# Layer norm of every stage: normalised rows made by ScalarE with a scale and a shift instead of by VectorE

## What is computed

```python
def _layernorm(x, axis=-1, eps=1e-05):
    m = jnp.mean(x, axis=axis, keepdims=True)
    v = jnp.var(x, axis=axis, keepdims=True)
    return (x - m) / jnp.sqrt(v + eps)

x = x + masked_attention(_layernorm(x))     # 16 heads of 16, T = 1024
x = x + ffn(_layernorm(x))                  # shared part of width 1024, 8 routed experts, top 2
x = x + gated_convolution(_layernorm(x))    # inner width 512, 4 taps
x = x + ffn(_layernorm(x))                  # the same weights again
x = x + selective_scan(_layernorm(x))       # 256 channels, 16 states
x = x + moe(_layernorm(x))                  # 16 routed experts, top 2
x = x + grouped_query_attention(_layernorm(x))  # 32 query heads, 4 key heads of 128
x = x + moe(_layernorm(x))
```

## Time and profile before

| | |
|---|---|
| median of 3 runs | 1946.65 us (1946.47 to 1948.49) |
| time of the profiled execution | 1946.17 us |
| its span, first to last instruction | 1944.3 us |
| PE busy | 1562.1 us (80%) |
| DVE busy | 1295.5 us (67%) |
| ACT busy | 932.3 us (48%) |
| POOL busy | 715.9 us (37%) |
| mean granted TensorE clock | 0.894 of 2.4 GHz |
| ACT's table loads (ACT_TABLE_LOAD) | 10, of 1.283 us each; none within a norm |

### The profile page before, as it was taken

How to read it: one execution, slowest core, us unless ns; L and a number is a source line. 1 busy time by engine, 2 the same in 40 slices (tenths; PEclk the granted TensorE clock), 3 DMA queues, 4 the chain that set the end, 5 groups by cost and what they waited for, 6 DMA issues and landing times. The chain is left out here.

```text
span 1944.3 us, 28391 instructions
## 1 busy us (share of the span) xinstructions
PE 1562.1 (80%) x9276; PEld 1214.6 (62%) x9286; DVE 1295.5 (67%) x2160; ACT 932.3 (48%) x2281; POOL 715.9 (37%) x735
## 2 busy tenths in 40 slices
PE   6899789878974655292769999999999999997372
PEld 4444568666851223281758888888888888885372
DVE  3665364766467998644647777777777778775743
ACT  2365335233524331251546666666666666663341
POOL 3011243324367764644832222222222222220743
PEclk9899799889987887595889999999999999999586
DMA  3320323222310001364000000000000000000443
GB/s 75 53 50 2 96 84 109 66 87 87 106 48 0 0 0 56 117 128 141 11 1 12 12 12 2 22 1 23 1 23 1 22 1 12 1 1 19 152 108 107
DMA packets 62059, 90.04 MB, mean 46 GB/s; under 512 B 10192, under 2 KB 44240, under 8 KB 61920
## 3 DMA queue, kind: packets, MB, share of 16 engines
q1 hardware_dynamic: 53664, 65.68, 11.4%
q0 software_dynamic: 8256, 22.56, 5.1%
HBM read 62.38 MB, written 19.40 MB: 42 GB/s over the span
## 5 line engine op out<-in xcount | busy, mean ns | idle before, releaser
L1294 DVE TENSOR_REDUCE gqa_neg_max<-acc 128x1 f32<-128x1024 f32 (+7 forms) x256 | 193.1, 754 | 173.2 <-PE acc L1403 172.1
L1180 ACT ACTIVATE gqa_probsT_high<-aux 128x512 fp32r<-128x512 f32 x288 | 172.0, 597 | 249.5 <-PE aux L1411 248.6
L1299 DVE TENSOR_TENSOR gqa_probsT_low<-aux,gqa_probsT_high 128x512 fp32r<-128x512 f32 x288 | 197.8, 687 | 29.8 <-ACT gqa_probsT_high L1180 25.6
L1189 ACT ACTIVATE gqa_probs<-acc,gqa_neg_max 128x1024 f32<-128x1024 f32 (+7 forms) x256 | 189.3, 739 | 29.6 <-DVE gqa_neg_max L1294 24.6
L1411 PE MATMUL aux<-ident,gqa_probs 128*128 128x128 f32 x1152 | 174.4, 274 | 0.0
L1087 POOL TENSOR_SCALAR gqa_q_scale<-gqa_q_scale 128x4 f32<-128x4 f32 x64 | 16.3, 255 | 381.0 <-ACT gqa_square L1124 380.7
L1422 PE MATMUL aux<-gqa_probsT_high,gqa_v_high 128*128 128x512 f32 x288 | 146.7, 509 | 1.0 <-DVE gqa_probsT_low L1299 1.0
L472 POOL DMA_INDIRECT f_xs<-tokens,f_slot_token x108 | 104.4, 967 | 108.4 <-PE aux L752 44.3
L1091 POOL TENSOR_TENSOR gqa_ln_xn<-gqa_ln_xn 128x512 f32<-128x512 f32 x64 | 82.2, 1285 | 147.0 <-DVE gqa_ln_xn L1219 146.9
L1434 PE MATMUL aux<-gqa_wo,gqa_oT 128*128 128x256 f32 x512 | 132.4, 381 | 4.4 <-DVE stream L1287 3.5
L1401 PE MATMUL acc<-gqa_k_low,gqa_q_high 128*128 128x512 f32 (+5 forms) x384 | 132.1, 344 | 0.0
(11 more groups left out here) (411 smaller groups left out, 4444.9 us busy)
## 6 DMA issues: line engine op xcount, KB each, us to landing
f_w<-in_f_up SPq DMA_DIRECT2D x64, 256.0 KB, 3.2
outputs_by_slot<-f_y_tile SPq DMA_DIRECT2D x108, 128.0 KB, 2.5
f_w<-in_f_down SPq DMA_DIRECT2D x64, 128.0 KB, 3.6
mat_qk<-mat_high SPq DMA_DIRECT2D x64, 64.0 KB, 2.3
tokens<-f_ln_xn SPq DMA_DIRECT2D x4, 1024.0 KB, 4.6
gqa_w_q<-in_g_wq SPq DMA_DIRECT2D x8, 512.0 KB, 3.6
gqa_wo<-in_g_wo SPq DMA_DIRECT2D x8, 512.0 KB, 3.8
mat_qk<-mat_low SPq DMA_DIRECT2D x32, 64.0 KB, 2.3
```

The lines of the kernel that those rows point to most:

```text
L1180: act.activation(probsT_high[:, u % RING, :], aux[:, u % 2, :], ACT.Copy).then_inc(cell_high_ready, 1)
L1189: act.activation(out, scores(n), ACT.Exp, bias=neg_max[:, j % (2 * JOBS):j % (2 * JOBS) + 1], accum_out=row_sum[:, n // 2 % 4, m, n % 2:n ...
L1294: dve.tensor_reduce(neg_max[:, j % (2 * JOBS):j % (2 * JOBS) + 1], scores(n), AXY, ALU.max, negate=True).then_inc(max_ready, 1)
L1299: dve.tensor_tensor(probsT_low[:, u % RING, :], aux[:, u % 2, :], probsT_high[:, u % RING, :].bitcast(F32), ALU.subtract).then_inc(cell_lo ...
```

## The change

The normalised tile is written by ACT, as `Identity(scale * x + bias)` with scale `rstd` and bias `shift` = -mean * rstd, both one value in each partition. POOL makes the shift: it negates the mean and multiplies it by `rstd`, two more small instructions for each pair (eight more for each layer). DVE's list becomes all statistics and then all low parts. ACT's list of the norm becomes, for each pair, the two `xn` tiles and then the `xnT_high` copy of the pair before. In the feed-forward layers ACT's `split(0)` moves from ahead of the norm to behind it. In masked attention ACT's norm moves ahead of the wait for the weights and their upper parts.

```diff
+        self.shift = sb("ln_shift", [P, NT])
+        self.mean_negated = sem("mean_negated")
+        self.shift_ready = sem("shift_ready")
...
-        def scale(q):
-            dve.wait_ge(self.rstd_ready, q + 1)
-            for t in (2 * q, 2 * q + 1):
-                dve.tensor_scalar(self.xn[:, t, :], c.x[:, t, :], self.mv[:, t, 0:1], self.rstd[:, t:t + 1],
-                                  ALU.subtract, ALU.mult).then_inc(self.xn_ready, 1)
...
-        for q in range(NT // 2 + 3):
-            if q < NT // 2:
-                statistics(q)
-            if 1 <= q < NT // 2 + 1:
-                scale(q - 1)
-            if q >= 3:
-                low(q - 3)
+        for q in range(NT // 2):
+            statistics(q)
+        for q in range(NT // 2):
+            low(q)
...
             pool.tensor_scalar(self.rstd[:, two], self.mv[:, two, 1], LN_EPS, None, ALU.add).then_inc(self.eps_added, 1)
+            pool.tensor_scalar(self.shift[:, two], self.mv[:, two, 0], -1.0, None, ALU.mult).then_inc(self.mean_negated, 1)
             pool.wait_ge(self.eps_added, q + 1)
             pool.tensor_tensor(self.rstd[:, two], self.rstd[:, two], self.core.minus_half[:, two],
                                ALU.pow).then_inc(self.rstd_ready, 1)
+            pool.wait_ge(self.rstd_ready, q + 1)
+            pool.wait_ge(self.mean_negated, q + 1)
+            pool.tensor_tensor(self.shift[:, two], self.shift[:, two], self.rstd[:, two], ALU.mult).then_inc(self.shift_ready, 1)
...
-        for q in range(NT // 2):
-            act.wait_ge(self.turned, q + 1)
-            act.activation(c.xnT_high[:, :, 2 * q * P:(2 * q + 2) * P],
-                           c.acc[:, q, :].rearrange("p (k t) -> p k t", k=DC), ACT.Copy).then_inc(self.high_ready, 1)
+        for q in range(NT // 2 + 1):
+            if q < NT // 2:
+                act.wait_ge(self.shift_ready, q + 1)
+                for t in (2 * q, 2 * q + 1):
+                    act.activation(self.xn[:, t, :], c.x[:, t, :], ACT.Identity, bias=self.shift[:, t:t + 1],
+                                   scale=self.rstd[:, t:t + 1]).then_inc(self.xn_ready, 1)
+            if q >= 1:
+                act.wait_ge(self.turned, q)
+                act.activation(c.xnT_high[:, :, 2 * (q - 1) * P:2 * q * P],
+                               c.acc[:, q - 1, :].rearrange("p (k t) -> p k t", k=DC), ACT.Copy).then_inc(self.high_ready, 1)
...
# feed-forward layers, ACT
+            norm.scalar(act)
             split(0)
-            norm.scalar(act)
...
# masked attention, ACT
+            norm.scalar(act)
             act.wait_ge(w_in, 48)
             for k in range(DC):
                 act.activation(w_high[:, k, :], w[:, k, :], ACT.Copy).then_inc(w_high_ready, 1)
-            norm.scalar(act)
```

## The result

The changed kernel took 1955.08 us (median of 6 runs, 1952.41 to 1957.37), the kernel before 1946.56 us (6 runs beside it, 1945.17 to 1948.49). The ratio is 1.0055, with a 95% interval of 1.0043 to 1.0067: 8.5 us slower by the medians, 10.7 by the ratio (8.4 to 13.0), where 1954.5 had been forecast. The profiled execution of the changed kernel took 1955.76 us; its span is 9.6 us longer than that of before.

The account below looks back on a forecast made before the run. The norm was taken to be on the path in all eight layers, with DVE its busiest engine. The layers' terms summed to +7.85 us on 1946.17, so 1954.0, forecast as 1954.5 because that execution lay 0.5 below the median; range 1948 to 1959.

Parts of the forecast that it names:

- Step 1: The norm by itself: POOL's pair period 1.5 us, fourth pair's transposes 0.95 us later, bounds 0.5 and 1.5.
- the term +0.95: Convolution: the layer loses what the norm alone loses, 0.95 us.
- The forecast of -1.1: Masked attention: with ACT's norm first, PE starts at 20.1 instead of 21.16, -1.1 us, bounds -1.5 and -0.6.
- Step 3: Scan: projection 2.95 us earlier, but POOL's third select holds a DVE tensor_scalar, so only -0.6 us is kept.
- Step 4: f3 and f4: the moved split delays POOL's first low part and DVE's expert-choice chain, +2.9 us for each layer.
- The two signs of a wrong forecast: The forecast is wrong if scan's L2322 runs at once or f3's L609 moves by under 2 us.
- the term +1.0: Grouped-query attention: +1.0 us through the weights' low parts up to PE's first projection, bounds 0.5 and 2.
- `Identity` brought no table load of its own: Rival on ACT's norm: `Identity` brings its own table loads, 1.3 us in seven layers, +17, 1963.6; chance 0.04.
- Collisions did not come cheaper: Rival for scan, f3 and f4: DVE and POOL collisions cost less than charged, sum +1.5, 1948.2; chance 0.15.
- second rival: Norm slower: POOL period 1.65, 0.6 us later in seven layers, one more f3/f4 collision; +12, 1958.6; chance 0.18.

Follow-up runs that it names:

- e5: The changed kernel with the negation of the means made by DVE behind its bn_aggr instead of by POOL; 1.0031 of the kernel before.
- e10: The changed kernel with POOL's rotary-table products waiting for DVE's four low parts of the key and value weights; 1.0052 of the kernel before.
- e6: The kernel before with POOL's memset in the scan waiting until all of the norm's tiles are scaled; 0.9996 of the kernel before.
- e2: The changed kernel with the scan's negation of a made by ACT instead of DVE; 1.0063 of the kernel before.
- e1: The changed kernel with the feed-forward layers' split(0) put back ahead of the norm on ACT; 1.0051 of the kernel before.
- e4: The kernel before with only the feed-forward layers' split(0) moved behind the norm on ACT, old norm kept; 1.0023 of the kernel before.
- e9: The kernel before, old norm, with masked attention's order changed, scan's memset held, its negation of a on ACT, and POOL's rotary-table products held; 1940.51 us, 0.9985.

## Why the forecast came out, and where it did not

With thirteen traces besides that of the kernel before, each layer can be compared over several traces in which nothing of it was edited but what the change does. Each length is the mean of three to seven traces; the last column is the prediction's term.

| layer | old (traces) | changed (traces) | difference | term |
|---|---|---|---|---|
| masked attention | 215.45 (4) | 212.86 (6) | -2.6 | -1.1 |
| f1 | 142.61 (6) | 143.24 (4) | +0.6 | +0.9 |
| convolution | 56.85 (7) | 58.91 (6) | +2.1 | +0.95 |
| f2 and scan together | 345.76 (3) | 346.16 (3) | +0.4 | +0.3 |
| f3 | 141.37 (6) | 144.23 (4) | +2.9 | +2.9 |
| grouped-query attention | 887.37 (5) | 892.69 (5) | +5.3 | +1.0 |
| f4 | 147.67 (6) | 150.50 (4) | +2.8 | +2.9 |
| sum | | | +11.5 | +7.85 |

+11.5 lies within both measured differences, 8.4 to 13.0 us beside the first trace and 9.7 to 17.9 on the third chip. The forecast's 7.85 is just under the first. The total was met in part by luck, because errors of both signs met: masked attention came out 1.5 shorter than its term, convolution and grouped-query attention 5.4 longer than theirs together, and all three lie outside the bounds that their terms had.

**Step 1, the norm: right in mechanism, 0.2 short.** POOL's period was put at 1.5 and is 1.56; ACT's tiles at 0.6 each and 1.1 the pair, and are 0.592 and 1.09. The estimate of 585 ns that was worked out from the prices of the Trainium skill ("ScalarE: Activation LUTs", What ACT_TABLE_LOAD costs) is borne out by the 592 of the trace. The fourth transposes came 1.16 later in convolution, where 0.95 was forecast, and 1.0 in f1, f2, f3 and f4, where it was 0.9. e5 shows that the bound was named rightly.

**Convolution: the term +0.95 was mis-sized, it measured +2.1.** The norm brought 1.16 of it, and the zeroing matmuls follow exactly that (t0+11.34 after, t0+10.19 before). Then the turn from 0.63 to 0.40 for a product of 512 columns comes after eight products instead of four (the granted clock goes from 0.50 to 1.00 at 378.4 after, 3.7 us behind the first product, and at 378.9 before, 1.9 behind it), and the first copy of `conv_xi` stands at t0+17.12 instead of t0+15.16, 1.96 later. In the seven traces of the old norm the turn comes after four or five products, in five of the six of the changed one after eight to ten; in the sixth, e10, it comes after four, and the layer takes 58.2. In e5 the turn came after three, and the whole layer was back to 57.2. So the norm's 1.16 is the change's in every trace, and the rest depends on where the turn falls. I had costed what stands behind the norm as shifted by as much as the norm, and that is not so where PE starts from idle.

**Masked attention: the step was right, the layer's time not.** The projection was forecast 13.1 after the first statistics and came at 13.11. The rest of the -4.0 is mostly PE's pace: 23 us into the layer the like product comes 2.4 earlier, 1.1 by the projection's start and 1.3 by the earlier turn from 0.63 to 0.40; the other 1.6 comes from stretches at a granted clock of 0.50 further on (44.4 to 51.2 and 61.5 to 75.1 us before, 57.5 to 74.6 after). The prediction had no term for it. The late turn, 6.1, stands only in the three traces of the old order whose projection is late (216.0 to 216.9 for the layer); the fourth, whose weights landed early, has 212.4, and the ten traces of the new order have 211.4 to 214.3. The forecast of -1.1 took one arrival of the weights as given, and in the old order that arrival is a draw of the execution.

**Step 3, scan: right in mechanism, and its size in part by luck.** L2326 ran 2.43 instead of 0.18 and ended at 589.18, with POOL's third select at 589.14. The cast behind it gained 0.99 of the 2.84 that the projection gained (0.6 of 2.95 forecast). The rule of the Trainium skill ("SBUF — State Buffer", Who interferes with whom), that whoever starts first has the shared ports for its whole instruction, was borne out by this and by e6, where the hold ended with the select in progress and not with the three. The scan's further gain in the first pair of traces was not the change's: f2 and scan together are 0.4 longer, beside the forecast's 0.3. But the 1.0 at the loop's start is not simply kept: e2 moved that start by another 1.3 and e6 the old kernel's by 2.2, and the two layers together came out 0.6 longer in the one trace and 0.3 shorter in the other. The term charged a shift at the cast as a shift of the layer.

**Step 4, f3 and f4: right.** The two signs of a wrong forecast (L2322 running at once, L609 of f3 moving by under 2 us) did not come. The first low part of POOL came 3.03 later (2.9 forecast), the product of `f_pick` 2.72 later, and the layers are 2.9 and 2.8 longer. e1 and e4 take it apart into 1.0 for the norm and 1.7 for the split. f4's +1.5 in the first pair is the least that the four traces show.

**Grouped-query attention: the term +1.0 was mis-sized, it measured +5.3.** The prediction had "bounds 0.5 and 2, because DVE's subtractions there may meet POOL's tables once more", and took hardly any of it (1.0 against the norm's 0.95). That is what failed here: e10 has the projection at + 14.57 without the collision, and the five traces of the changed kernel have it 4.3 to 6.4 later, while in the old kernel's five the collision cost nothing, 2.1 or 3.2 (+ 13.42, + 15.55 and + 16.62). POOL's tables start when a DMA lands (+ 11.1 to + 12.2 where neither SP's order nor a hold was edited), and DVE's four low parts start when the norm ends. The norm's 1.15 moves DVE into POOL's stretch: the four take 2.48 or 4.64 with the old norm, 5.70 or 6.78 with the new. The first row maximum comes at + 70.3 to + 72.4 with the old (mean 71.3) and at + 73.7 to + 76.8 with the new (75.0), 3.6 later. The hold of e10 takes the collision away and leaves 1.15. The remaining 1.7 stands in the loop; layers of one kind differ by 4 to 6.6 us. It goes with the granted clock: by the traces' clock records the layer spends 54 us (44 to 61) at 0.5 in the five old traces and 61 (58 to 67) in the five changed ones, and the two shortest layers of all, 883.4 in e9 and 883.8 in e6, have the least, 40 and 44. One such stretch is at a granted clock of 0.5, 1.2 GHz, in the changed kernel's first trace; the first trace of before has it at 1.00 (window, length, PE busy and count, granted clock, DMA share, GB/s; before, then after):

```profile
1000.00:1005.00 5.00, 3.33 (x20) 1.00 0.00 0
1005.00:1010.00 5.00, 4.91 (x28) 1.00 0.00 0
```

```profile
1000.00:1005.00 5.00, 3.77 (x12) 0.50 0.00 0
1005.00:1010.00 5.00, 5.00 (x16) 0.51 0.00 0
```

Across it the delay against the trace of before grew from 3.5 to 7.2 us, by the starts of like products (995.02 and 998.52, then 1002.53 and 1009.73). That the later start causes the fall was not tried.

**The rivals.** `Identity` brought no table load of its own: the only one at the norm's line is the first of the program, at 7.12, which stood at the weights' copy before, and ended 1.36 ahead of the first tile. Collisions did not come cheaper; in grouped-query attention they came dearer than any rival had them. The sum of the second rival, +12, holds its six tenths in seven layers and not the collision in f3 and f4 that its text adds; with 0.7 for each it would be about +13.5.

## What to carry to other kernels

Taking work from the busiest engine of a stage gains nothing where the relief is paid for with a longer chain of small dependent steps on another: the norm here got slower because POOL, with four instructions in place of two, came to set its period, and ACT, which took the tiles, stood close behind it with its own list. Before moving a start by one microsecond, look at which stretches of DVE and POOL lie next to it: a DVE subtraction with both inputs in SBUF that begins beside a POOL tensor operation costs two to three times its length, and in grouped-query attention a one-line hold of the less urgent of the two removed it. And take several traces of the unchanged kernel before reading a difference of 2 to 4 us in one layer.

## What the runs showed of the hardware that was not expected

- One POOL select holds a DVE `tensor_scalar` and a cast from SBUF to SBUF until it ends (0.18 to 2.43, 0.68 to 3.10), and leaves a cast out of PSUM alone (1.21 in both cases). Between two selects DVE gets in.
- A subtraction of 128x1024 out of SBUF takes 1.23 where it starts ahead of POOL's products, even if only by 0.25 us (e10), and 2.28 or 3.35 where it starts behind one.
- The turn of PE from 0.63 to 0.40 us for 512 columns came 3.1, 3.5 or 4.8 us behind the first projection of masked attention in traces of one and the same code and start (+ 13.1), and 6.1 behind it in the three traces where it started at + 14.1 or later. The granted clock of the windows read 1.00 through 21 to 27 us in the trace of before, while the products took 0.63; there the rows' lengths tell the level, and the window does not (the first clock record of that trace stands at 27.3).
- Two executions of one kernel drew different collisions from a DMA that landed 0.17 us earlier (+ 11.25 instead of + 11.42), and the first row maximum was 2.8 us later in the one.
